# Layer 1's ternary feed-forward stage: loops written out, transposed x two steps ahead, small operations in groups of four tiles

## The reference

```
s_x  = 127 / max(|n|, 1e-5)                      # max over the 256 entries
xq   = round(n * s_x)                            # small integers
g    = (xq @ Tgate) * mean|Wgate| / s_x ; u the same with Tup
h    = silu(g) * u                               # 1024 wide
s_h  = 127 / max(|h|, 1e-5)                      # max over the 1024 entries
y    = (round(h * s_h) @ Tdown) * mean|Wdown| / s_h
x    = x + tanh(gate) * y
```

## Time and profile before

| | |
|---|---|
| device time, median of 3 runs | 2710.25 us (2708.65 to 2712.22) |
| profiled execution: its own time | 2702.28 us |
| its span, granted TensorE clock | 2700.5 us, 0.962 |
| the stage, first DVE instruction to end of the last addition | 859.22 to 1038.24 us |
| busy over the span | PE 90%, DVE 60%, POOL 50%, ACT 48% |

### The profile page before, as it was taken

How to read it: one execution, slowest core, us unless ns; L and a number is a source line. 1 busy time by engine, 2 the same in 40 slices (tenths; PEclk the granted TensorE clock), 3 DMA queues, 4 the chain that set the end, 5 groups by cost and what they waited for, 6 DMA issues and landing times. The chain is left out here.

```text
span 2700.5 us, 43042 instructions
## 1 busy us (share of the span) xinstructions
PE 2420.3 (90%) x12786; PEld 1429.2 (53%) x12787; DVE 1612.7 (60%) x3262; ACT 1288.6 (48%) x2559; POOL 1351.7 (50%) x2270
## 2 busy tenths in 40 slices
PE   6997999999996775799999999899969975999997
PEld 3554666766663553344445344355546663666664
DVE  5884664655554874687877868488866644212121
ACT  4664443544443773466566566566653431222221
POOL 3665663233445774224353434466875304656663
PEclk9998999999998998899999999999988986999999
DMA  4001000000100003222141231100004151222222
GB/s 137 6 1 67 1 0 1 1 0 1 47 1 16 1 0 76 62 66 71 31 111 44 54 87 37 48 24 24 1 1 164 47 197 24 45 46 47 43 47 28
DMA packets 85449, 115.14 MB, mean 43 GB/s; under 512 B 15432, under 2 KB 64432, under 8 KB 83600
## 3 DMA queue, kind: packets, MB, share of 16 engines
q1 hardware_dynamic: 66736, 92.36, 11.4%
q0 software_dynamic: 18528, 20.50, 4.7%
HBM read 77.92 MB, written 34.64 MB: 42 GB/s over the span
## 5 line engine op out<-in xcount | busy, mean ns | idle before, releaser
L3411 ACT ACTIVATE L2S_pT<-L2S_t_ps 128x512 f32<-128x512 f32 (+3 forms) x768 | 356.2, 491 | 212.8 <-PE L2S_t_ps L3235 204.3
L3475 DVE TENSOR_REDUCE L2S_mx<-L2S_s_ps 128x1 f32<-128x768 f32 (+7 forms) x384 | 350.5, 951 | 111.0 <-PE L2S_s_ps L3158 110.2
L3235 PE MATMUL L2S_t_ps<-L2S_q,L2S_k 98*128 98x512 bf16 (+3 forms) x768 | 248.4, 334 | 16.3 <-DMA L2S_q<-L2S_mrow 6.4
L3715 POOL TENSOR_SCALAR_AFFINE_SELECT L2S_pT<-L2S_pT 128x128 f32<-128x128 f32 x512 | 150.8, 309 | 170.0 <-ACT L2S_pT L3411 165.6
L3157 PE MATMUL L2S_s_ps<-L2S_k,L2S_q 96*128 96x512 bf16 (+3 forms) x768 | 198.5, 331 | 16.3 <-DVE L2S_mx L3475 7.5
L622 POOL TENSOR_TENSOR L_prob<-L_prob,L_rc 128x616 f32<-128x616 f32 x64 | 82.2, 1285 | 231.5 <-DVE L_rc L555 231.5
L4091 DVE TENSOR_TENSOR L3B_h<-L3B_si,L3B_u_ps 128x512 f32<-128x512 f32 x71 | 48.9, 688 | 237.4 <-PE L3B_u_ps L4034 237.4
L4008 POOL DMA_INDIRECT out<-L3B_y,L3F_rows x71 | 114.7, 1616 | 134.6 <-DVE L3B_y L4097 120.1
L3235 PEld LDWEIGHTS L2S_t_ps<-L2S_q,L2S_k 98*128 98x128 bf16 x768 | 72.8, 97 | 194.9 <-ACT L2S_pT L3411 129.0
L3335 PE MATMUL L2S_o_ps<-L2S_pT,L2S_v 128*32 128x512 f32 (+3 forms) x1536 | 165.4, 504 | 0.0
L319 PE MATMUL L_scores<-weights,L_xT 128*128 128x308 f32 x512 | 143.2, 423 | 2.3 <-ACT L_xT L442 1.6
(11 more groups left out here) (540 smaller groups left out, 5803.0 us busy)
## 6 DMA issues: line engine op xcount, KB each, us to landing
qk_parts<-L2S_part SPq DMA_DIRECT2D x90, 128.0 KB, 2.4
L2S_q<-qk_parts SPq DMA_DIRECT2D x32, 192.0 KB, 3.4
L2S_k<-qk_parts SPq DMA_DIRECT2D x30, 192.0 KB, 3.4
L2S_q<-qk_parts SPq DMA_DIRECT2D x32, 128.0 KB, 3.2
L3F_w<-in_L_gu SPq DMA_DIRECT2D x8, 512.0 KB, 6.9
weights<-in_L_w SPq DMA_DIRECT2D x8, 512.0 KB, 9.0
out<-x_sb SPq DMA_DIRECT2D x8, 512.0 KB, 3.3
expert_rows<-L_xn SPq DMA_DIRECT2D x8, 512.0 KB, 3.0
```

What stands on the lines that cost most here:

```text
L3235: nc.tensor.matmul(o[:, lo:512], k6[:, q % 2, j, kt * P:(kt + 1) * P], q6[:, q % 2, c, j, lo:512], start=True, stop=True).then_inc(s["t_fu ...
L3411: nc.scalar.activation(pT[:, st % SLOTS, j, lo:512], t_ps[j % 2][:, lo:512], ACT.Exp, scale=SK).then_inc(s["exp_done"], 1)
L3475: nc.vector.tensor_reduce(dst, src, AX.X, ALU.max).then_inc(s["mx_done"], 1)
L3715: nc.gpsimd.affine_select(out=edge, in_=edge, compare_op=ALU.is_ge, fill=0.0, base=0, pattern=[[1, P]], channel_multiplier=-1).then_inc(s[ ...
```

## The change

The whole stage is written out: no loop, no register addresses, and the waits are on constants. Small operands have a column for each of the 32 tiles, xn has eight buffers and xT four. In step `at`, PE and ACT still run `widen` and `silu` of tile at-3, but `turn_x` and `copy_x` (still last in their orders) are of tile at-1, so that they are ahead of their use by a whole step more. The DVE order becomes `quantise` of tile at-1, statistics (9 tiles before use in the steady part), normalising (4 tiles), `multiply`. POOL does `rstd` and `scale_x` for groups of tiles (1, 3, then 4 at a time). `scale_h` has four operations in place of five and comes first in POOL's step; `add` is last and of tile at-7. An activation on one column stands ahead of ACT's first step.

```diff
+    GROUPS = [range(0, 1), range(1, 4)] + [range(a, a + 4) for a in range(4, T, 4)]
+    LAST = T + 7
+    STATS_AT = {0: (0, 1, 2, 3), 1: (8, 9), 2: (10, 11)} | {t - 9: (t,) for t in range(12, T)}
+    NORM_AT = {0: (0,), 1: (1, 2, 3), 2: (4, 5), 3: (6, 7)} | {t - 4: (t,) for t in range(8, T)}
+    RSTD_AT = {0: (0, 1), 1: (2,)} | {4 * n - 10: (n,) for n in range(3, len(GROUPS))}
+    SCALE_AT = {0: (0,), 1: (1,), 3: (2,)} | {4 * n - 5: (n,) for n in range(3, len(GROUPS))}
+    group_of = {t: n for n, g in enumerate(GROUPS) for t in g}
...
+        stat, mv, ve, rs = sb("stat", [P, T, 6]), sb("mv", [P, T, 2]), sb("ve", [P, T]), sb("rs", [P, T])
+        xn, xq, xT = sb("xn", [P, 8, D]), sb("xq", [P, 2, D]), sb("xT", [P, 4, KD, P], BF16)
+        am, ax, ix, gs, us, us127 = (sb(n, [P, T]) for n in ("am", "ax", "ix", "gs", "us", "us127"))
...
+        def steps(*phases):
+            for at in range(1, LAST):
+                for phase, behind in phases:
+                    if 0 <= at - behind < T:
+                        phase(at - behind)
...
-            def turn_x(t, q):
-                p = q % 2
+            def turn_x(t):
                 pe.wait_ge(s["xq_done"], t + 1)
+                if t:
+                    pe.wait_ge(s["xT_free"], t)
...
+                for o, n, full, free in ((g_ps, "gate", "g_full", "silu_done"), (u_ps, "up", "u_full", "h_done")):
+                    if t:
+                        pe.wait_ge(s[free], t)
...
 
-            none = lambda t, p: None
-            pipelined(pe, [none, none, turn_x, widen, none, turn_h, narrow], unroll=4, order=(3, 5, 6, 2))
+            steps((widen, 3), (turn_h, 5), (narrow, 6), (turn_x, 1))
...
-            act.sem_inc(s["hq_done"], 2)
-            act.sem_inc(s["silu_done"], 1)
...
+            def copy_x(t):
+                act.wait_ge(s["xT_full"], t + 1)
+                if t >= 4:
+                    act.wait_ge(s["u_full"], t - 3)
...
-            none = lambda t, p: None
-            pipelined(act, [none, none, copy_x, silu, quantise, copy_h, result], unroll=4, order=(3, 4, 5, 6, 2))
+                if t >= 2:
+                    act.wait_ge(s["x_done"], t - 1)
+                nc.scalar.activation(res[:, t % 2, :], o_ps[:, 0:D], ACT.Identity, scale=ev[:, t:t + 1]).then_inc(s["o_free"], 1)
+
+            nc.scalar.activation(ready[:], chip.neghalf[:, 0:1], ACT.Silu)
+            steps((silu, 3), (quantise, 4), (copy_h, 5), (result, 6), (copy_x, 1))
...
-            link = Links(dve, s["dve_step"], [1, 1, 0, 1, 0, 0, 0])
...
-                nc.vector.bn_aggr(mv[:, p, :], stat[:, p, :]).then_inc(s["stats_done"], 1)
-                link.leave()
-
...
-                dve.wait_ge(s["ix_done"], t + 3)
-
-                dve.wait_ge(s["xT_full"], t + 1)
...
+            step = Count(s["dve_step"])
+
+            def ahead(stats, norms):
+                for t in stats:
+                    nc.vector.bn_stats(stat[:, t, :], tile(t)).then_inc(s["dve_step"], 1)
+                    measured = step.up()
+                if stats:
+                    dve.wait_ge(s["dve_step"], measured)
+                    for t in stats:
+                        nc.vector.bn_aggr(mv[:, t, :], stat[:, t, :]).then_inc(s["stats_done"], 1)
+                for t in norms:
+                    dve.wait_ge(s["rstd_done"], group_of[t] + 1)
+                    if t >= 8:
+                        dve.wait_ge(s["xq_done"], t - 7)
+                    nc.vector.tensor_scalar(xn[:, t % 8, :], tile(t), mv[:, t, 0:1], rs[:, t:t + 1], ALU.subtract, ALU.mult).then_inc(s["dve_step"], 1)
+                    normed = step.up()
+                if norms:
+                    dve.wait_ge(s["dve_step"], normed)
+                    for t in norms:
+                        nc.vector.tensor_reduce(am[:, t:t + 1], xn[:, t % 8, :], AX.X, ALU.max, apply_absolute_value=True).then_inc(s["xn_done"], 1)
+
+            def quantise(t):
+                dve.wait_ge(s["ix_done"], group_of[t] + 1)
+                if t >= 2:
+                    dve.wait_ge(s["xT_full"], t - 1)
+                nc.vector.tensor_scalar(xq[:, t % 2, :], xn[:, t % 8, :], ix[:, t:t + 1], ROUND, ALU.mult, ALU.add).then_inc(s["xq_done"], 1)
+
+            def multiply(t):
+                dve.wait_ge(s["silu_done"], t + 1)
                 dve.wait_ge(s["u_full"], t + 1)
-                nc.vector.tensor_tensor(h[:, p, :], h[:, p, :], u_ps[:], ALU.mult).then_inc(s["h_done"], 1)
-                dve.wait_ge(s["h_done"], t + 2)
-                link(nc.vector.tensor_reduce(ah[:, p:p + 1], h[:, p, :], AX.X, ALU.max, apply_absolute_value=True))
-                dve.sem_inc(s["ah_done"], 1)
-                link.leave()
-
-            none = lambda t, p: None
-            pipelined(dve, [stats, normalise, quantise, multiply, none, none, none], unroll=4)
+                nc.vector.tensor_tensor(h[:, t % 2, :], h[:, t % 2, :], u_ps[:], ALU.mult).then_inc(s["h_done"], 1)
+                dve.wait_ge(s["h_done"], t + 1)
+                nc.vector.tensor_reduce(ah[:, t:t + 1], h[:, t % 2, :], AX.X, ALU.max, apply_absolute_value=True).then_inc(s["ah_done"], 1)
+
+            ahead((0,), ())
+            ahead((1, 2, 3), ())
+            ahead((), (0,))
+            ahead((4, 5, 6, 7), ())
+            for at in range(1, LAST):
+                if at - 1 < T:
+                    quantise(at - 1)
+                ahead(STATS_AT.get(at, ()), NORM_AT.get(at, ()))
+                if 0 <= at - 3 < T:
+                    multiply(at - 3)
 
...
+            step = Count(s["pool_step"])
+
+            def link(ins):
+                ins.then_inc(s["pool_step"], 1)
+                pool.wait_ge(s["pool_step"], step.up())
+
+            def rstd(n):
+                c = cols(n)
+                pool.wait_ge(s["stats_done"], c.stop)
+                link(nc.gpsimd.tensor_scalar(ve[:, c], mv[:, c, 1], 1e-5, None, ALU.add))
+                nc.gpsimd.tensor_tensor(rs[:, c], ve[:, c], chip.neghalf[:, c], ALU.pow).then_inc(s["rstd_done"], 1)
+
+            def scale_x(n):
+                c = cols(n)
+                pool.wait_ge(s["xn_done"], c.stop)
+                link(nc.gpsimd.tensor_scalar(ax[:, c], am[:, c], 1e-5, 1.0 / 127.0, ALU.max, ALU.mult))
+                nc.gpsimd.tensor_scalar(gs[:, c], ax[:, c], wmean[:, 0:1], None, ALU.mult)
+                link(nc.gpsimd.tensor_scalar(us[:, c], ax[:, c], wmean[:, 1:2], None, ALU.mult))
+                nc.gpsimd.tensor_scalar(us127[:, c], us[:, c], 127.0, None, ALU.mult)
+                nc.gpsimd.tensor_tensor(ix[:, c], ax[:, c], minus1[:, 0:c.stop - c.start], ALU.pow).then_inc(s["ix_done"], 1)
+
+            def scale_h(t):
+                pool.wait_ge(s["ah_done"], t + 1)
+                link(nc.gpsimd.tensor_scalar(most[:, t:t + 1], ah[:, t:t + 1], us[:, t:t + 1], 1e-5, ALU.mult, ALU.max))
+                link(nc.gpsimd.tensor_tensor(ai[:, t:t + 1], most[:, t:t + 1], minus1[:, 0:1], ALU.pow))
+                nc.gpsimd.tensor_tensor(ev[:, t:t + 1], most[:, t:t + 1], out_scale[:], ALU.mult)
+                nc.gpsimd.tensor_tensor(s2[:, t:t + 1], ai[:, t:t + 1], us127[:, t:t + 1], ALU.mult).then_inc(s["s2_done"], 1)
+
+            def add(t):
+                pool.wait_ge(s["o_free"], t + 1)
+                nc.gpsimd.tensor_tensor(tile(t), tile(t), res[:, t % 2, :], ALU.add).then_inc(s["x_done"], 1)
+
...
+            rstd(0)
             link(nc.gpsimd.tensor_tensor(wmean[:, 2:3], wmean[:, 2:3], gate, ALU.mult))
-            link.start = link.k
...
-                link.enter(1, t)
-                pool.wait_ge(s["xn_done"], t + 1)
-                chip.settle(pool)
-
-                link(nc.gpsimd.tensor_scalar(ax[:, q:q + 1], am[:, p:p + 1], 1e-5, 1.0 / 127.0, ALU.max, ALU.mult))
...
-            def scale_h(t, q):
-                p = q % 2
-                link.enter(3, t)
-                pool.wait_ge(s["ah_done"], t + 1)
-                link(nc.gpsimd.tensor_tensor(ah[:, p:p + 1], ah[:, p:p + 1], us[:, q:q + 1], ALU.mult))
-                chip.settle(pool)
-                link(nc.gpsimd.tensor_scalar(ah[:, p:p + 1], ah[:, p:p + 1], 1e-5, 1.0 / 127.0, ALU.max, ALU.mult))
-                link(nc.gpsimd.tensor_tensor(ai[:, p:p + 1], ah[:, p:p + 1], minus1[:], ALU.pow))
-                link(nc.gpsimd.tensor_tensor(ev[:, q:q + 1], ah[:, p:p + 1], wmean[:, 2:3], ALU.mult))
-                link(nc.gpsimd.tensor_tensor(s2[:, p:p + 1], ai[:, p:p + 1], us[:, q:q + 1], ALU.mult))
-                pool.sem_inc(s["s2_done"], 1)
-                link.leave()
...
-            none = lambda t, p: None
-            pipelined(pool, [rstd, scale_x, none, scale_h, none, none, add], unroll=4)
-
+            link(nc.gpsimd.tensor_scalar(out_scale[:], wmean[:, 2:3], 1.0 / 127.0, None, ALU.mult))
+            scale_x(0)
+            rstd(1)
+            for at in range(1, LAST):
+                if 0 <= at - 4 < T:
+                    scale_h(at - 4)
+                for n in SCALE_AT.get(at, ()):
```

(44 more changed lines are left out.)

98 lines of the change are left out of this document (20 added, 78 removed).

## The result

The changed kernel took 2677.02 us (median of 4 runs, 2673.22 to 2681.6), the kernel before, run beside it, 2709.45 (2704.5 to 2712.22): a ratio of 0.9891, 95% interval 0.9877 to 0.9905. The profiled execution has 2678.13 us, its span is 2676.4.

What follows compares the result with a forecast made beforehand. POOL's 5.04 us chain, just above a 4.83 ring, bounds the kernel; DVE would at 4.1, then a ring at 3.95. Last silu 24.1 earlier, plus 0.4, less 1.0: gain 23.5, from 2710.25 to 2687 us, range 2680 to 2699.

Steps and rivals of the forecast that it cites:

- DVE's step: DVE's own sum of measured distances, 4.09, taken as 4.1 us: the new bound of every step with statistics.
- the tail behind the last silu: After the last silu: the same chain with one POOL operation less, 0.4 us gained.
- the 1.0 us taken off for a slow start: At the start PE is slower, silu to multiply 1.60 instead of 1.14 for two tiles: 1.0 us lost.
- the lock between DVE and POOL: DVE tensor_scalar held by POOL instructions; forecast not held. Rival: 4.8 + 3 us less gain, 2694.6 us, chance 0.08.
- the crowded steps: One step in four, with scale_x on POOL: scale_h, hq and silu 0.4 late, costing 0.5 us together.
- Two bounds close together: In the kernel before, POOL's chain sets the step at 5.04 us, with a ring just below at 4.83.
- The chain of POOL: Twelve small linked POOL operations that wait for no other engine: 5.04 us a step, forecast to fall to 3.15.
- the ring of ACT and PE: Silu to hq 1.01, hq to copy_x 2.30, copy_x to next silu 1.52 (waiting for PE): 4.83 us a step.
- bn_stats to am 1.10: First term of DVE's sum, from 1007.78 to 1008.88 in the profile before: 1.10 us of each step.
- The ring over two steps: Silu through multiply, ah, POOL and hq to a later silu: 7.92 us, bounding the last eleven steps at 3.95.
- the ends given for the stage: Best and worst term sizes: a gain of 28.6 us at one end, 13.3 us at the other.
- The fetch: Rival: fetching the written-out stage's instructions, 11 more packets, costs up to 30 us: 2717 us, chance 0.05.

Runs made afterwards that it cites:

- x_late: Changed kernel with turn_x and copy_x of tile at-2 again, groups and written-out form kept: 2702.5 us, ratio 0.9980, stage 177.69 us.
- ones: Changed kernel with groups of one tile for rstd and scale_x, x still two steps ahead: 2698.17 us, ratio 0.9975, stage 174.16 us.
- pause: Changed kernel with DVE's wait for its own ah and the separate ah_done increment put back: 2684.3 us, ratio 0.9922, stage 157.40 us.
- add_early: Changed kernel with POOL's add moved right behind scale_h, ahead of scale_x and rstd: 2673.56 us, ratio 0.9878, stage 150.30 us.

## Why the prediction was right, and where it was wrong

The mechanism of the bounds was right, and the sum was too small: 23.5 us where the stage gained 27.6. The terms that were mis-sized are DVE's step (4.1 us, measured 3.96: 2.7 us over 19 steps), the tail behind the last silu (0.4 us of gain, measured 1.9) and the 1.0 us taken off for a slow start (measured nothing). One error went the other way: the lock between DVE and POOL, priced in the crowded steps at 0.5 us by another cause, cost 2.3 there. The rest of the miss is in the total and not in the stage: the two medians differ by 32.4 us, 4.8 more than the stage.

**Two bounds close together** was right, and it is the main point. The chain of POOL (5.04) and the ring of ACT and PE (4.83) were 4% apart. With only the groups (x_late) the step fell to 4.83, with only the earlier x (ones) to 4.8; together they fell to 3.96. The stages are 1.3 and 4.9 us shorter with one of the two and 27.6 with both. All three are written out, and the longer starts of the first two are in these figures; the steps show the effect without them.

**The new bound** was named rightly, DVE in every step with statistics, and its step was sized at 4.1 where it is 3.96. The term is "bn_stats to am 1.10": it is 938.38 - 937.39 = 0.99, as bn_aggr now starts 0.46 behind bn_stats and started 0.58 behind it before:

```profile
1008.36 0.18 DVE L2100 BATCH_NORM_AGGREGATE L1F_mv<-L1F_stat 128x2 f32<-128x6 f32 x1 [0.15 <-DVE L1F_stat L2098]
```

I took that wait of 0.15 us for the engine's own. Why it went is not shown. The whole 0.14 us makes 2.7 us over 19 steps.

**The lock** was wrong. I read from a power on one column that DVE is not held by POOL, and gave its rival 0.08. The changed kernel shows xq held by an addition for 0.57 us in each of four steps, and among the last ones a norm for 0.42 and an xq for 0.17: 2.9 us in all, and deferring the additions gave back 3.1. In all of these, and in six more in the run named pause, the held instruction ends 0.14 to 0.16 us behind the addition. A power on one or four columns held no xq; an addition on 256 columns did. The Trainium skill (SBUF — State Buffer, Who interferes with whom) was right on the addition, and the 3 us worked out by it for xq were near the 2.4 measured; on the norms beside the powers (4.8 us by its rule) it was not, none was held: they took 0.40 us. Of the 3.1, 2.3 us lie in the four steps with statistics (0.57 each), where I had charged 0.5.

**The ring over two steps**: 7.92 forecast, 4.17 + 3.56 = 7.73 measured, and 43.05 us for the last eleven steps against 43.45.

**The end and the start** failed by more than the steps did, net of the lock. The slower PE of the start was charged with 1.0 us on top of a start worked out in full: the start came out 0.4 us shorter than that, not 1.0 longer. And the tail, from the last silu to the last addition, is 12.32 us where it was 14.21: 1.9 less, not 0.4. 0.5 of it is the shorter chain to hq. The other 1.4 is PE. These are the last `turn_h` and the `narrow` behind it, before and after:

```profile
1031.86 1.68 PE L2034 MATMUL L1F_hT_ps<-ident,L1F_hq 128*128 128x128 f32 x8 [2.69 <-ACT L1F_hT L2079]
...
1033.33 1.92 PE L2042 MATMUL L1F_o_ps<-weights,L1F_hT 128*128 128x256 bf16 x8
```

```profile
1008.21 1.06 PE L2046 MATMUL L1F_hT_ps<-ident,L1F_hq 128*128 128x128 f32 x8 [1.38 <-ACT L1F_hT L2084]
...
1009.11 1.04 PE L2054 MATMUL L1F_o_ps<-weights,L1F_hT 128*128 128x256 bf16 x8
```

Before, PE had paused 2.69 us ahead of them, and the granted clock fell to the lower of its two levels while they ran (0.50 from 1033 to 1035 us): eight transposes took 1.68 us and eight `narrow` matmuls 1.92. Now the clock stays at 1.00 and they take 1.06 and 1.04. I had priced the tail as if only instruction counts could change it. What made the clock fall is not shown: the pause is shorter now (1.38 us), but pauses of one length went both ways. Ahead of the group before these, the changed kernel (first row) and add_early (second) paused alike:

```profile
1004.90 1.06 PE L2046 MATMUL L1F_hT_ps<-ident,L1F_hq 128*128 128x128 f32 x8 [2.11 <-ACT L1F_hT L2084]
```

```profile
1002.06 1.58 PE L2046 MATMUL L1F_hT_ps<-ident,L1F_hq 128*128 128x128 f32 x8 [2.10 <-ACT L1F_hT L2084]
```

The first ran at 1.00; in add_early the granted clock is 0.50 from 1003 to 1005 us. All three profiles of the kernel before have the drop in the last two groups, and no profile of the changed kernel has it, so the 1.4 us repeat; that they come with the change for a reason is not shown.

So 23.5 becomes 27.6: the last silu 25.7 us earlier and not 24.1 (2.7 from the shorter steps, 0.4 from the start and 0.4 from the last eleven steps, less 1.8 for crowded steps charged with 0.5 instead of 2.3; these make 1.7 of the 1.6), 1.9 in the tail and not 0.4, and no 1.0 to take off. That the 27.6 us lie within the ends given for the stage has some luck in it: the lock hid 1.8 us of terms that were too cautious, and with the additions deferred the stage gains 30.8, beyond the better end of 28.6.

**What the range missed.** 27.6 us lies within the ends that I gave for the stage (13.3 to 28.6), but 2677 lies outside 2680 to 2699, because the two medians differ by 32.4. A gain of 27.6 off the 2710.25 of before would have been 2682.6, inside it. The later medians of before are 2706.18 (23 runs), 2705.32 (9) and 2703.45 (17), not 2710.25, and those of the changed kernel 2677.02 and 2674.22. I allowed nothing for the scatter of a median of three. The measured ratio is kinder than the medians: its interval, 0.9877 to 0.9905, is a gain of 25.7 to 33.3 us and holds the stage's 27.6. Whether some 2 to 3 us more are gained outside the stage stays open: nine of ten timed comparisons gained 2 to 8 us more by their medians than by their stages, the one named pause 2.5 less, and before against itself differed by 3.7. By the intervals of the ratios, the stage's gain lies inside nine of the ten; only that of x_late (0.9969 to 0.9992) asks for more than its 1.3 us. No experiment here tells a small gain outside the stage from this scatter.

**The fetch** did not show: the stage drew 7 packets on q8, as worked out, and no matmul or DVE instruction has a pause that would be one. The waits put down to "issue" are all of weight loads, up to 2.4 us in this stage and up to 2.9 in that of before, the longest of them in the tail, where PE waits for ACT. That writing out costs nothing is argued from that; that it brings 0.2 us a step was measured only together with the shorter `scale_h`.

## What to carry to other kernels

Where an engine's chain waits for nobody and a ring between others is a few per cent shorter, take both off at once, and do not judge either change by what it brings alone: each alone brought 1.3 and 4.9 us of 27.6 here. Then size the next bound from the new order's own gaps, and ask which streaming operation on POOL now falls beside a tensor_scalar on DVE; here moving it one step on gave 3.1 us (2666.79 and 2670.44 us; the version that also filled DVE's wait took 2672.05 with a stage 0.3 us shorter, and the intervals of their ratios overlap, so these two are not told apart). A stage's length in the trace told 1 us apart (151.40 and 151.42 against 150.30) where medians could not tell 3.

## What the hardware showed that was not expected

An addition of 128x256 on POOL stretched a tensor_scalar of 128x256 on DVE from 0.34 to 0.91 us; a power on 128x4, running for 1.04 us beside the same instruction, did not. In the other direction a power on one column took 0.65 us in place of 0.56 when a norm began 0.2 us behind it and its usual end fell inside the norm; it ended about where the norm did:

```profile
937.73 0.65 POOL L2168 TENSOR_TENSOR L1F_ai<-L1F_most,L1F_minus 128x1 f32<-128x1 f32 x1
...
937.94 0.40 DVE L2111 TENSOR_SCALAR L1F_xn<-x_sb,L1F_mv,L1F_rs 128x256 f32<-128x256 f32 x1
```

PE's pace in a stage's tail is not given by its instructions alone: eight transposes took 1.06 us at a granted clock of 1.00, and 1.6 to 1.9 us where it fell to 0.50 while they ran. A pause of 2.69 us came before one such drop and one of 2.10 before another, but one of 2.11 did not bring it.
